# A table of relations made for two blocks at a time, one in each half of the array's rows, with four block buffers on the way out

## The chip, the cores and the metric

The kernel runs on one core of a Trainium2 chip. The metric is the device time of one execution in microseconds (us), lower is better; times given for a kernel are the median of several runs.

## What is computed

A graph network of four layers on 12500 nodes of 64 features and 400000 edges (sorted by target). Each layer normalises the nodes, takes the positive part, passes messages along the edges and adds the result to the nodes. The change touches what stands between the second layer and the third:

```python
h = jnp.maximum(_layernorm(x, axis=-1), 0.0)
x = x + _L1_gnn_ref(h, edge_attr_64, edge_index, M_W, M_b, U_W, U_b)   # ends in relu([H, Z] @ U_W.T + U_b)
h = jnp.maximum(_layernorm(x, axis=-1), 0.0)
x = x + _L2_gnn_ref(h, L2_gnn_weight, src, dst, edge_type_16)
# _L2: for r in range(16): msg = msg + h[src] * (etypes == r)[:, None] @ weight[r];  out = segment_sum(msg, dst)
```

The kernel does not multiply per edge. It makes a table with a row for every node and relation, `h @ weight[r]` for the 16 values of r, in device memory (HBM), and the third layer then gathers the row (node, relation) of each edge.

## The kernel before

Nodes are held in 98 blocks (`NB`) of 128 nodes, one node to a partition (`P` = 128), 64 words (`D`) a block. The program is a row of stages with a barrier between them: `starts_stage`, `record_stage` (which also makes the first layer's table), `gather_layer` for the first layer, `message_table`, `gather_layer` for the second, **`update_table`**, `gather_layer` for the third, and the stages of the fourth layer. Within a stage every engine runs an instruction list of its own, in the order in which it is written, and the lists are tied together by semaphores only. No scheduler moves anything.

`update_table` (line 865) has two parts. The first finishes the second layer and normalises: TensorE turns the sums and h of seven blocks (`turn`, L990 and L991, which write the two column halves, that is PSUM partitions 0 to 63 and 64 to 127), ScalarE copies them to `ct` (L950), TensorE multiplies by the update weights (`product`, L998), VectorE adds the bias, takes the positive part and adds to x (`update`, L907, L910), and VectorE and ScalarE normalise in chunks of 14 blocks (L925 to L940, L971, L977).

The second part is the loop over the 98 blocks that makes the table, which is the one that is changed:

- TensorE, `turn_h` (L1006): every seven blocks (`SUB`), seven matmuls with the identity turn h into `ps_t`, PSUM partitions 0 to 63.
- ScalarE, `turned_h` (L956): copies these 64x896 words to `ct[s % 2]`.
- TensorE, `table_block` (L1016): two matmuls a block with the 64 features as contraction, on array rows 0 to 63, give 1024 columns (16 relations of 64) in `ps_m[n % 2]`, 1024 words of PSUM, after both engines have taken the block before last out of it.
- `take_product`: ScalarE copies the first 512 columns (L961) and VectorE the other 512 (L915) to `tb[n % 2]`, each after the transfer of the block before last has landed (`s_out`).
- SP (L896): one transfer of 128x1024 words, 512 KB, to the table for each block, after both copies. Its queue holds nothing else in this part.

The weights `w` (64x1024 words) are loaded once, by SP at L892, ahead of the stage's first matmul. An f32 matmul has two records in the profile, so a block's two matmuls are four records of L1016.

## Time and profile before

| | |
|---|---|
| median of 3 runs | 22004.11 us (21988.52, 22004.11, 22110.69) |
| profiled execution | 22027.31 us, of which the span is 22025.5 us |
| mean granted TensorE clock over the span | 0.55 |
| busy: PE, DVE, ACT, POOL | 44%, 41%, 12%, 72% |
| DMA | 1898.85 MB, mean 86 GB/s |

The span is what lies between the first and the last instruction of the profiled execution. PE is TensorE's matmuls and PEld its weight loads, DVE is VectorE, ACT ScalarE, POOL GpSimd, SP SyncE, which issues most transfers. An engine's busy share is an average over all stages. "Idle before, released by" tells what an engine waited for; "issue" is time in which it waited for nothing that the profile shows. PEclk is the granted TensorE clock as a share of 2.4 GHz, 0.50 being 1.2 GHz. The stage `update_table` stands at 12577 to 12904 us of the span.

### The profile page before, as it was taken

The numbers are of one execution on the slowest core, as the hardware profiler recorded it, in microseconds if no ns is written. First come the engines' busy times: TensorE is split into PE (matmuls) and PEld (weight loads), VectorE is DVE, ScalarE is ACT, GpSimd is POOL, SyncE is SP. The second block draws the span as 40 slices with busy tenths as digits, with TensorE's granted clock in tenths as the row PEclk, the third lists the DMA queues.
The fourth block names the chain that finished last, engine by engine and source line by source line (L and its number), as shares of the span: only waits on it lengthen the run. The fifth ranks groups of instructions, "written<-read, shape, count | busy, mean of one in ns | idle before, by whom it ended". The sixth has DMA issues, their size and how long they took to land. (4 is left out here: it accounts for less than half of the span.)

```text
span 22025.5 us, 196973 instructions
## 1 busy us (share of the span) xinstructions
PE 9713.1 (44%) x45757; PEld 6967.4 (32%) x45758; DVE 9017.1 (41%) x22705; ACT 2705.0 (12%) x6341; POOL 15954.0 (72%) x16948
## 2 busy tenths in 40 slices
PE   2777776433333335666666653333333111111146
PEld 1333333233333334333333433333332000000046
DVE  7777777644444443222222232222223222222246
ACT  4000000000000000000000010000000222222256
POOL 2777777777777776777777647777776777777776
PEclk7555555555555555666666665555555555555578
DMA  3333332222222222222222132222222333333366
GB/s 109 98 99 98 99 97 82 72 63 63 61 62 63 63 62 58 60 63 63 63 60 63 46 134 63 61 63 63 63 61 59 111 110 111 110 112 111 109 208 232
DMA packets 1023243, 1898.85 MB, mean 86 GB/s; under 512 B 356036, under 2 KB 464484, under 8 KB 1009716
## 3 DMA queue, kind: packets, MB, share of 16 engines
q1 hardware_dynamic: 497556, 1233.35, 17.2%
q0 software_dynamic: 513696, 661.43, 11.3%
q10 hardware_dynamic: 11904, 3.04, 0.1%
q8 instruction: 38, 0.62, 0.0%
q14 instruction: 49, 0.40, 0.0%
HBM read 1385.02 MB, written 511.62 MB: 86 GB/s over the span
## 5 line engine op out<-in xcount | busy, mean ns | idle before, releaser
L1124 POOL DMA_INDIRECT arena<-table,arena x6464 | 6116.1, 946 | 2340.2 <-issue 1891.1
L1236 PE MATMUL psum<-arena 128*128 128x64 f32 x19392 | 3981.9, 391 | 5145.0 <-DMA arena<-table,arena 4548.8
L1236 PEld LDWEIGHTS psum<-arena 128*128 128x128 f32 x19392 | 3909.6, 304 | 5717.8 <-issue 5717.8
L1175 DVE TENSOR_TENSOR arena<-arena,psum 128x64 f32 x9696 | 2154.3, 222 | 8056.4 <-PE psum L1236 6827.4
L707 POOL DMA_INDIRECT rec<-arena x3125 | 3008.3, 963 | 1341.6 <-issue 949.4
L1320 POOL DMA_INDIRECT rec<-arena x3232 | 3109.5, 962 | 1069.2 <-issue 975.2
L1124 POOL DMA_INDIRECT arena<-ptable,arena x3232 | 3058.1, 946 | 1086.7 <-issue 985.7
L1403 PE MATMUL psum<-arena 128*128 x3232 | 589.1, 362 | 3512.0 <-DVE arena L1350 3433.1
L484 PE MATMUL psum<-arena 128*128 128x196 bf16 (+1 forms) x4375 | 1377.9, 428 | 1270.0 <-DVE arena L615 1270.0
L1222 PE MATMUL psum<-arena 128*128 128x512 f32 x808 | 838.0, 1141 | 1620.6 <-DMA arena<-ptable,arena 1620.6
L1403 PEld LDWEIGHTS psum<-arena 128*128 128x128 bf16 x3232 | 350.2, 108 | 3750.7 <-issue 3661.2
L1340 DVE TENSOR_TENSOR arena<-arena 128x136 f32<-128x136 f32 x404 | 122.1, 302 | 3058.3 <-DMA arena<-rec 3058.2
L615 DVE TENSOR_TENSOR arena<-psum,arena 128x392 f32<-128x392 f32 x1875 | 920.0, 491 | 345.6 <-PE psum L484 224.4
L484 PEld LDWEIGHTS psum<-arena 128*128 128x128 bf16 x4375 | 366.5, 115 | 2195.5 <-DVE arena L615 1820.0
L1154 DVE TENSOR_TENSOR arena<-psum,arena 128x1024 f32<-128x1024 f32 x808 | 984.5, 1219 | 23.4 <-issue 22.4
L1223 PE MATMUL psum<-arena 128*128 128x512 f32 x808 | 752.7, 1035 | 0.0
L1370 ACT ACTIVATE arena<-arena 128x1024 bf16<-128x1024 bf16 x404 | 463.4, 1147 | 2314.4 <-DMA arena<-lanes 2314.4
L620 DVE TENSOR_REDUCE arena<-arena 128x10 f32<-128x980 f32 x625 | 734.1, 1175 | 21.5
L1481 POOL TENSOR_SCALAR arena<-arena 128x128 bf16<-128x128 bf16 x880 | 641.3, 745 | 135.5 <-ACT arena L1493 133.2
L1222 PEld LDWEIGHTS psum<-arena 128*128 128x128 f32 x808 | 202.3, 311 | 1682.0 <-DMA arena<-ptable,arena 1517.9
L607 DVE TENSOR_TENSOR arena<-psum,arena 128x980 bf16<-128x980 f32 x625 | 729.9, 1168 | 0.0
L1198 ACT ACTIVATE arena<-psum 128x512 f32<-128x512 f32 x404 | 241.9, 599 | 3817.9 <-PE psum L1223 3817.9
(216 smaller groups left out, 11243.6 us busy)
## 6 DMA issues: line engine op xcount, KB each, us to landing
arena<-rec SPq DMA_DIRECT2D x303, 1408.0 KB
arena<-rec SPq DMA_DIRECT2D x440, 488.0 KB, 4.9
arena<-in_edge SPq DMA_DIRECT2D x625, 232.0 KB, 2.6
arena<-rec SPq DMA_DIRECT2D x404, 352.0 KB, 3.3
arena<-table,arena POOLq DMA_INDIRECT x6464, 2.4
arena<-lanes SPq DMA_DIRECT2D x101, 1024.0 KB
rec<-arena POOLq DMA_INDIRECT x6357, 2.3
table<-arena SPq DMA_DIRECT2D x196, 512.0 KB
```

The lines of the kernel that those rows point to most:

```text
L484: return nc.tensor.matmul(to, identb, one_hots, start=False, stop=False, skip_group_check=True)
L615: v.tensor_tensor(prod[g][:, 2 * n * WIDE:2 * n * WIDE + w], run[:, 0:w], buf[g][:, 2 * n * WIDE:2 * n * WIDE + w], ALU.mult).then_inc(s_s ...
L620: v.tensor_reduce(posf[:, g * CG * KEYS:(g + 1) * CG * KEYS], prod[g].rearrange("p (t w) -> p t w", w=NB), AX.X, ALU.add).then_inc(s_red, 1)
L707: nc.gpsimd.indirect_dma_start(rec, bass.IndirectOffsetOnAxis(ap=stage[g][:, j:j + 1], axis=0), recs[g][:, j * RW:(j + 1) * RW], None).the ...
L1124: nc.gpsimd.indirect_dma_start(rows[q][:, j * D:(j + 1) * D], None, tab, bass.IndirectOffsetOnAxis(ap=idx[:, j, field:field + 1], axis=0)) ...
L1154: v.tensor_tensor(ones, iotas, lanes, ALU.is_equal).then_inc(s_hot[q], 1)
L1175: v.tensor_tensor(block_sum, block_sum, ps[q % SB][:, j * D:(j + 1) * D], ALU.add).then_inc(s_add[j], 1)
L1222: nc.tensor.matmul(ps_q[q % 2], ident, rows[q], start=True, stop=False)
L1223: nc.tensor.matmul(ps_q[q % 2].rearrange("p (j f) -> p j f", f=D), ident, recs[q].rearrange("p (j w) -> p j w", w=RW)[:, :, R_Q:RW], start ...
L1236: last = nc.tensor.matmul(ps[q % SB][:, j * D:(j + 1) * D], hot[q % SB][:, j * P:(j + 1) * P], rows[q][:, j * D:(j + 1) * D], start=True, ...
L1320: nc.gpsimd.indirect_dma_start(slots, bass.IndirectOffsetOnAxis(ap=goal[q][:, j:j + 1], axis=0), rows[q][:, j * ROW:(j + 1) * ROW], None). ...
L1403: last = nc.tensor.matmul(ps_m[q % 2][:, j * 256:j * 256 + HW], hot_t[q % HB][:, j * P:(j + 1) * P], hparts[:, bass.ds(ats[j] * PARTS, HW) ...
```

## The change

Blocks are taken in pairs, seven blocks apart (block `n` and block `n + 7` of the same chunk of 14). The first block of a pair ("side 0") has its turned h on partitions 0 to 63 and the weights there, the second ("side 1") on partitions 64 to 127, where a second load puts the same weights. A unit `u` is one half (512 columns) of the rows of both blocks: two matmuls, one on array rows 0 to 63, the other on rows 64 to 127, into two banks of PSUM, each with its own semaphore `s_mm[side]`. Three such units fit in PSUM (`TRIO`), one of them where `ps_u` was, for which TensorE now waits at `s_pos`. ScalarE copies all of side 0 and VectorE all of side 1, one 128x512 copy a unit each. There are four block buffers `tb`, two for each side, and SP sends both blocks of a pair one after the other, every second unit. `turn_h` turns 14 blocks at a time, in the two column halves, and ScalarE's copy of them is 128x896.

```diff
--- before.py
+++ after.py
@@ -874,14 +874,17 @@
     uw, ub, w = b.take(D), b.take(D), b.take(width)
     ct = [b.take(SUB * P) for _ in range(2)]
     pos = [b.take(SUB * D) for _ in range(2)]
-    tb = [b.take(width) for _ in range(2)]
+    tb = [b.take(width) for _ in range(4)]
     assert b.at <= ARENA - NB * D
-    names = ("w", "t", "ct", "u", "pos", "x", "total", "mid", "sq", "var", "std", "rs", "h", "th", "ht", "mm")
-    s_w, s_t, s_ct, s_u, s_pos, s_x, s_total, s_mid, s_sq, s_var, s_std, s_rs, s_h, s_th, s_ht, s_mm = (sem("t2_" + n) for n in names)
-    s_ca, s_cv, s_out = ([sem(f"t2_{n}{k}") for k in range(2)] for n in ("ca", "cv", "out"))
+    names = ("w", "t", "ct", "u", "pos", "x", "total", "mid", "sq", "var", "std", "rs", "h", "th", "ht", "ca", "cv")
+    s_w, s_t, s_ct, s_u, s_pos, s_x, s_total, s_mid, s_sq, s_var, s_std, s_rs, s_h, s_th, s_ht, s_ca, s_cv = (sem("t2_" + n) for n in names)
+    s_mm = [sem(f"t2_mm{k}") for k in range(2)]
+    s_out = [sem(f"t2_out{k}") for k in range(4)]
     ps_t = psum[:, 0:SUB * P]
     ps_u = [psum[:, 1024 + 512 * k:1024 + 512 * k + SUB * D] for k in range(2)]
-    ps_m = [psum[:, 2048 + 1024 * k:3072 + 1024 * k] for k in range(2)]
+    TRIO = 3
+    ps_m = [[psum[:, 1024 * u + 512 * k:1024 * u + 512 * (k + 1)] for k in range(2)] for u in range(1, TRIO + 1)]
+    PAIRS_K = NB // 2
     bias = ub.rearrange("p (o f) -> p o f", o=1).to_broadcast([P, SUB, D])
 
     with nc.Block() as block:
@@ -889,13 +892,15 @@
         def _(sp):
             sp.dma_start(uw, a["uw"]).then_inc(s_w, 16)
             sp.dma_start(ub, a["ub"].to_broadcast([P, D])).then_inc(s_w, 16)
-            sp.dma_start(w[0:D, :], a["w2"]).then_inc(s_w, 16)
-            for n in range(NB):
-                sp.wait_ge(s_ca[n % 2], n // 2 + 1)
-                sp.wait_ge(s_cv[n % 2], n // 2 + 1)
-                sp.dma_start(dest[n * P:(n + 1) * P, :], tb[n % 2]).then_inc(s_out[n % 2], 16)
             for k in range(2):
-                sp.wait_ge(s_out[k], 16 * (NB // 2))
+                sp.dma_start(w[k * D:(k + 1) * D, :], a["w2"]).then_inc(s_w, 16)
+            for t in range(PAIRS_K):
+                for k, taken in ((0, s_ca), (1, s_cv)):
+                    n = t // SUB * CH + k * SUB + t % SUB
+                    sp.wait_ge(taken, 2 * t + 2)
+                    sp.dma_start(dest[n * P:(n + 1) * P, :], tb[t % 2 * 2 + k]).then_inc(s_out[t % 2 * 2 + k], 16)
+            for k in range(4):
+                sp.wait_ge(s_out[k], 16 * (-(-(PAIRS_K - k // 2) // 2)))
 
         @block.vector
         def _(dve):
@@ -909,12 +914,14 @@
                 dve.wait_ge(s_pos, s + 1)
                 v.scalar_tensor_tensor(x[:, at], pos[s % 2], 0.0, x[:, at], ALU.max, ALU.add).then_inc(s_x, 1)
 
-            def take_product(n):
-                dve.wait_ge(s_mm, n + 1)
-                wait_earlier(dve, s_out[n % 2], n // 2 * 16)
-                v.tensor_copy(tb[n % 2][:, half:], ps_m[n % 2][:, half:]).then_inc(s_cv[n % 2], 1)
-
-            dve.wait_ge(s_w, 48)
+            def take_product(u):
+                t, c = u // 2, u % 2 * half
+                dve.wait_ge(s_mm[1], u + 1)
+                if c == 0:
+                    wait_earlier(dve, s_out[t % 2 * 2 + 1], t // 2 * 16)
+                v.tensor_copy(tb[t % 2 * 2 + 1][:, c:c + half], ps_m[u % TRIO][1]).then_inc(s_cv, 1)
+
+            dve.wait_ge(s_w, 64)
             update(0)
             update(1)
             for k in range(CHUNKS + 2):
@@ -939,8 +946,8 @@
                     dve.wait_ge(s_rs, k - 1)
                     v.scalar_tensor_tensor(rows_of(h, k - 2, CH), rows_of(h, k - 2, CH), 0.0, spread(rs, k - 2),
                                            ALU.max, ALU.mult).then_inc(s_h, 1)
-            for n in range(NB):
-                take_product(n)
+            for u in range(NB):
+                take_product(u)
 
         @block.scalar
         def _(act):
@@ -949,16 +956,19 @@
                 wait_earlier(act, s_u, s - 1)
                 nc.scalar.copy(ct[s % 2], ps_t).then_inc(s_ct, 1)
 
-            def turned_h(s):
-                act.wait_ge(s_th, s + 1)
-
-                wait_earlier(act, s_mm, (s - 1) * SUB)
-                nc.scalar.copy(ct[s % 2][0:D, :], ps_t[0:D, :]).then_inc(s_ht, 1)
-
-            def take_product(n):
-                act.wait_ge(s_mm, n + 1)
-                wait_earlier(act, s_out[n % 2], n // 2 * 16)
-                nc.scalar.copy(tb[n % 2][:, 0:half], ps_m[n % 2][:, 0:half]).then_inc(s_ca[n % 2], 1)
+            def turned_h(k):
+                act.wait_ge(s_th, k + 1)
+
+                for side in range(2):
+                    wait_earlier(act, s_mm[side], (k - 1) * CH)
+                nc.scalar.copy(ct[k % 2], ps_t).then_inc(s_ht, 1)
+
+            def take_product(u):
+                t, c = u // 2, u % 2 * half
+                act.wait_ge(s_mm[0], u + 1)
+                if c == 0:
+                    wait_earlier(act, s_out[t % 2 * 2], t // 2 * 16)
+                nc.scalar.copy(tb[t % 2 * 2][:, c:c + half], ps_m[u % TRIO][0]).then_inc(s_ca, 1)
 
             turned(0)
             turned(1)
@@ -976,10 +986,10 @@
                     act.wait_ge(s_var, k)
                     nc.scalar.activation(rs[:, at], var[:, at], ACT.Sqrt, bias=epsc, scale=1.0 / D).then_inc(s_std, 1)
             turned_h(0)
-            for n in range(NB):
-                if n % SUB == SUB - 2 and n // SUB + 1 < SUBS:
-                    turned_h(n // SUB + 1)
-                take_product(n)
+            for u in range(NB):
+                if u % CH == CH - 4 and u // CH + 1 < CHUNKS:
+                    turned_h(u // CH + 1)
+                take_product(u)
 
         @block.tensor
         def _(pe):
@@ -998,37 +1008,39 @@
                     last = nc.tensor.matmul(ps_u[s % 2][:, j * D:(j + 1) * D], ct[s % 2][:, j * P:(j + 1) * P], uw, start=True, stop=True)
                 last.then_inc(s_u, 1)
 
-            def turn_h(s):
-                pe.wait_ge(s_h, s // 2 + 1)
-                wait_earlier(pe, s_ht, s)
+            def turn_h(k):
+                pe.wait_ge(s_h, k + 1)
+                wait_earlier(pe, s_ht, k)
                 for j in range(SUB):
-                    n = s * SUB + j
-                    last = nc.tensor.matmul(ps_t[0:D, j * P:(j + 1) * P], h[:, n * D:(n + 1) * D], ident, start=True, stop=True)
+                    for side in range(2):
+                        n = k * CH + side * SUB + j
+                        last = nc.tensor.matmul(ps_t[side * D:(side + 1) * D, j * P:(j + 1) * P], h[:, n * D:(n + 1) * D], ident, start=True, stop=True)
                 last.then_inc(s_th, 1)
 
-            def table_block(n):
-                s, j = n // SUB, n % SUB
-                if j == 0:
-                    pe.wait_ge(s_ht, s + 1)
-                wait_earlier(pe, s_ca[n % 2], n // 2)
-                wait_earlier(pe, s_cv[n % 2], n // 2)
-                for c in (0, half):
-                    last = nc.tensor.matmul(ps_m[n % 2][:, c:c + half], ct[s % 2][0:D, j * P:(j + 1) * P], w[0:D, c:c + half],
-                                            start=True, stop=True)
-                last.then_inc(s_mm, 1)
-
-            pe.wait_ge(s_w, 48)
+            def table_unit(u):
+                k, j, c = u // CH, u % CH // 2, u % 2 * half
+                if u % CH == 0:
+                    pe.wait_ge(s_ht, k + 1)
+                wait_earlier(pe, s_ca, u - TRIO + 1)
+                wait_earlier(pe, s_cv, u - TRIO + 1)
+                for side in range(2):
+                    rows = slice(side * D, (side + 1) * D)
+                    nc.tensor.matmul(ps_m[u % TRIO][side], ct[k % 2][rows, j * P:(j + 1) * P], w[rows, c:c + half],
+                                     start=True, stop=True).then_inc(s_mm[side], 1)
+
+            pe.wait_ge(s_w, 64)
             turn(0)
             for s in range(SUBS):
                 if s + 1 < SUBS:
                     turn(s + 1)
                 product(s)
             pe.wait_ge(s_ct, SUBS)
+            pe.wait_ge(s_pos, SUBS)
             turn_h(0)
-            for n in range(NB):
-                table_block(n)
-                if n % SUB == SUB - 3 and n // SUB + 1 < SUBS:
-                    turn_h(n // SUB + 1)
+            for u in range(NB):
+                table_unit(u)
+                if u % CH == CH - 6 and u // CH + 1 < CHUNKS:
+                    turn_h(u // CH + 1)
 
 
 def parts_stage(nc, sem, b, epsc, x, acc, h, hparts):
```

The order of TensorE's instructions in the table loop, which sets how often it turns and how many matmuls stand between. L1006 turns h and L1016 makes the table; the first row is the last product of the part before. Before:

```order
L998 MATMUL psum<-arena 128x64 x14
L1006 MATMUL psum<-arena 64x128 x7
L1016 MATMUL psum<-arena 128x512 x10
L1006 MATMUL psum<-arena 64x128 x7
L1016 MATMUL psum<-arena 128x512 x14
L1006 MATMUL psum<-arena 64x128 x7
L1016 MATMUL psum<-arena 128x512 x14
```

And with the change, where L1017 turns h and L1028 makes the table:

```order
L1008 MATMUL psum<-arena 128x64 x14
L1017 MATMUL psum<-arena 64x128 x14
L1028 MATMUL psum<-arena 128x512 x18
L1017 MATMUL psum<-arena 64x128 x14
L1028 MATMUL psum<-arena 128x512 x28
L1017 MATMUL psum<-arena 64x128 x14
L1028 MATMUL psum<-arena 128x512 x28
```

The turns are half as many and twice as long, and the second of them comes after 9 units (18 matmuls) where it came after 5 blocks (10 matmuls). The number of table matmuls is the same, 196.

The order of ScalarE's instructions from the last square roots of the normalisation on. L956 copies the turned h, L961 one half of a block. Before:

```order
L971 ACTIVATE arena<-arena 128x896
L977 ACTIVATE arena<-arena 128x14 x2
L956 COPY arena<-psum 64x896
L961 COPY arena<-psum 128x512 x5
L956 COPY arena<-psum 64x896
L961 COPY arena<-psum 128x512 x7
```

And with the change, L964 and L971 in their places:

```order
L981 ACTIVATE arena<-arena 128x896
L987 ACTIVATE arena<-arena 128x14 x2
L964 COPY arena<-psum 128x896
L971 COPY arena<-psum 128x512 x10
L964 COPY arena<-psum 128x896
L971 COPY arena<-psum 128x512 x14
```

The copies of products are as many as before, and those of the turned h half as many with twice the partitions. The first of them stands behind the same square root.

## Rows read from the trace of the kernel before

**Rows 1.** Timeline, start of the loop: start us, us, engine, line, operation [idle before].

```profile
12695.26 0.88 ACT L956 COPY arena<-psum 64x896 f32<-64x896 f32 x1
...
12696.20 16.57 PE L1016 MATMUL psum<-arena 64*128 64x512 f32 x19 [6.35 <-ACT arena L956]
...
12700.79 10.56 SPq L896 DMA_DIRECT2D table<-arena  x4
...
12713.56 3.16 PE L1006 MATMUL psum<-arena 128*64 128x128 f32 x14
```

**Rows 2.** Timeline, last transfer of the table and first of the next stage.

```profile
12900.62 0.33 SPq L896 DMA_DIRECT2D table<-arena  x1
12904.28 1.50 SPq L1110 DMA_DIRECT2D arena<-rec  x3
```

**Rows 3.** First line of the page.

```profile
span 22025.5 us, 196973 instructions
```

**Rows 4.** The page's costliest group: count, busy, mean ns, idle before and why.

```profile
L1124 POOL DMA_INDIRECT arena<-table,arena x6464 | 6116.1, 946 | 2340.2 <-issue 1891.1
```

**Rows 5.** Windows: length, busy PE, PEld, DVE, ACT, POOL; PEclk, DMA share, GB/s.

```profile
12696.20:12716.50 20.30, 20.30 (x34) 9.33 (x34) 4.79 (x8) 2.93 (x5) 0.00 (x0) 0.50 0.32 129
12716.50:12900.80 184.30, 183.03 (x542) 86.01 (x540) 64.32 (x93) 65.67 (x106) 0.00 (x0) 1.00 0.65 262
2000.00:3000.00 1000.00, 711.11 (x2242) 370.97 (x2242) 740.04 (x1678) 96.06 (x538) 759.39 (x791) 0.50 0.32 98
21932.50:22000.50 68.00, 67.58 (x425) 47.98 (x423) 43.83 (x45) 30.78 (x36) 9.15 (x4) 1.00 0.10 21
```

**Rows 6.** Timeline of TensorE in the steady part of the loop.

```profile
12784.73 1.74 PE L1006 MATMUL psum<-arena 128*64 128x128 f32 x14
12786.41 12.28 PE L1016 MATMUL psum<-arena 64*128 64x512 f32 x28
...
12800.29 12.28 PE L1016 MATMUL psum<-arena 64*128 64x512 f32 x28
...
12883.82 15.71 PE L1016 MATMUL psum<-arena 64*128 64x512 f32 x36
```

**Rows 7.** Lines from 12560 to 12905: count, busy, mean ns, idle before by releaser.

```profile
L915 DVE COPY arena<-psum 128x512 f32<-128x512 f32 x98 | 67.8, 692 | 135.2 <-DMA table<-arena 69.8 <-PE psum L1016 65.4
```

**Rows 8.** Timeline, two issues of SP, and two copies that waited for them.

```profile
12763.59 0.33 SPq L896 DMA_DIRECT2D table<-arena  x1
...
12764.83 0.33 SPq L896 DMA_DIRECT2D table<-arena  x1
...
12766.40 0.59 ACT L961 COPY arena<-psum 128x512 f32<-128x512 f32 x1 [1.76 <-DMA table<-arena]
...
12767.58 0.59 ACT L961 COPY arena<-psum 128x512 f32<-128x512 f32 x1 [0.59 <-DMA table<-arena]
```

**Rows 9.** DMA queues from 12780 to 12880: packets, MB, share of 16 engines.

```profile
q1 hardware_dynamic: 7232, 26.35, 64.9%
```

**Rows 10.** Timeline of TensorE, column halves at full clock in the stage's first part.

```profile
12608.79 0.27 PE L990 MATMUL psum<-arena 128*64 128x128 f32 x1
12608.80 0.27 PE L991 MATMUL psum<-arena 128*64 128x128 f32 x1
12608.90 0.27 PE L990 MATMUL psum<-arena 128*64 128x128 f32 x1
```

**Rows 11.** Lines from 12560 to 12905, copies of turned blocks; timeline, last bias addition.

```profile
L950 ACT COPY arena<-psum 128x896 f32<-128x896 f32 x14 | 12.6, 899 | 41.9 <-PE psum L991 41.9
L956 ACT COPY arena<-psum 64x896 f32<-64x896 f32 x14 | 12.6, 899 | 9.3 <-PE psum L1006 9.3
...
12687.20 0.62 DVE L907 TENSOR_TENSOR arena<-psum,arena 128x448 f32<-128x448 f32 x1 [5.12 <-PE psum L998]
```

**Rows 12.** DMA queue from 98 to 148; GB/s in 40 slices from 12796 to 12806.

```profile
q1 hardware_dynamic: 10465, 18.18, 101.5%
...
GB/s 377 426 410 230 393 410 442 410 393 49 0 0 197 410 393 426 393 279 426 410 393 393 410 66 33 0 0 0 0 0 0 213 410 393 410 393 279 0 246 393
```

## The prediction

> **What bounds the kernel now.** I looked first at how much of the program the change can reach, then at what paces that piece. The loop that makes the table of relations in `update_table` begins with ScalarE's copy of the first turned h at 12695.26 [rows 1] and ends with the next stage's first load at 12904.28 [rows 2]: 209.0 us, 0.95% of the span of 22025.5 us [rows 3]. The layer after it is one of the two whose indirect loads are the page's costliest group, 946 ns each on POOL and "issue" as the main reason for its idle time [rows 4], and nothing there is touched. The two gather layers and the scatter stage run as before, so the whole result lies inside these 209.0 us, and a change of 0.5% (110 us, about what a measurement of this kernel can tell from none) would take more than half of them.
>
> Inside, TensorE is the pace. In the stretch at full clock it is busy 183.03 of 184.30 us [rows 5]. A block is two f32 matmuls of 512 columns, each recorded twice, so four records: 28 records last 12.28 us and 36 last 15.71, which is 0.429 us a record and 1.72 us a block; the seven turns of h between cost 1.74 us, and 12786.41 to 12800.29 makes 13.88 us for seven blocks, 1.98 us a block [rows 6]. At the start the granted clock is 0.50 (1.2 GHz) until just after the first turn [rows 5], and a record takes twice that, 0.857 us (19 of them in 16.57, with the last one's tail) [rows 1]. VectorE's copy is 0.69 us a block [rows 7] and ScalarE's 0.59 [rows 8], so neither is near. The transfers are nearer: in 100 us they moved 26.35 MB and took 64.9% of the 16 engines [rows 9]. The waits put half of the copies' idle time on the table's DMA [rows 7], because a block's buffer is reused every second block, but a TensorE that is busy throughout does not wait for those copies: the DMA is next in line, not first.
>
> **The change, part by part.** *Row halves.* Work is now counted in units: one unit is a half row of 512 columns for two blocks, block A on array rows 0 to 63 and block B on rows 64 to 127, into different banks. There are 98 units with 196 matmuls, as many as before. If the two run at once a unit takes 0.857 us at full clock; if in turn, 1.71. No row here has two row halves. The nearest are the column halves of L990 and L991: they start 0.01 us apart and the pair advances by 0.11 us, no more than one 128-column record alone needs at that clock (1.74 us for 14 records of L1006) [rows 10, 6]. I take them as simultaneous and keep 1.71 as the other end.
>
> *Turns.* 14 turns of 7 matmuls become 7 turns of 14, as column pairs; by the column pairs a turn costs about 1.7 us, so six inside the loop instead of thirteen. TensorE then needs 14 x 0.857 + 1.7 = 13.7 us for 14 units, 0.98 us a unit.
>
> *Copies.* Each engine still makes 98 copies of 128x512, now each for its own block, so 0.69 us a unit is VectorE's need. ScalarE's copy of the turned h grows from 64 to 128 partitions; L956 and L950, of either height, both take 0.90 us [rows 11], so nothing is added, and there are seven fewer, on an engine with slack.
>
> *Transfers, the new pace.* The 98 transfers of 512 KB stay. From [rows 9], 26.35 MB at 64.9% is 406 GB/s at full use, 1.29 us a transfer. That exceeds TensorE's 0.98 and VectorE's 0.69. Does the queue stay full with four buffers? A transfer's buffer is free 2.8 us after its issue (issued 12763.59 and 12764.83, copies let go at 12766.40 and 12767.58) [rows 8]. Those two were issued 1.24 us apart and let their copies go 1.18 apart, so transfers overlap. The second of a pair starts some 0.33 us (one issue) after the first and queues behind its packets, 1.29 - 0.33 = 0.96 us more. The buffer is refilled by two copies, 1.38 us, plus 0.1 to the next issue. The ring is 2.8 + 0.96 + 1.38 + 0.1 = 5.24 us for two pairs, 2.62 us a pair; the packets alone want 2.58. They nearly coincide, and I take 2.63, so 49 pairs are 128.9 us. The ends: packets alone, 126.4, and for the upper end the longest full-use writes in this trace, 18.18 MB in 50 us or 364 GB/s with the engines full [rows 12], 1.44 us a transfer or 141.1 us.
>
> By the Trainium skill ("DMA: Bandwidth & Descriptors", Specifications) the HBM limit of a core is about 358 GB/s: 1.46 us a transfer, and the sum would be 143.5 us for the 98. Its neighbour here is the 364 GB/s; against it, the table's own packets show slices of 410 GB/s within a block [rows 12], and those 50 us are of packets of 1.7 KB, so I stay with 406.
>
> *Start and end.* The first two units take as long as the first block now if the halves run at once (two times two records at 0.857), so the first issue stays at 12700.79, 5.53 us after 12695.26 [rows 1]. While the clock is still at 1.2 GHz a pair takes 3.41 us on TensorE, 0.8 more than the transfers want. Two or three such pairs cost 2 us; bounds 0 and 5 (six pairs, until 12716.5). At the end, last issue to next stage is 12900.62 to 12904.28, 3.66 us, of which 1.29 is the transfer: 2.37 fixed [rows 2].
>
> *Added waits.* TensorE now waits for VectorE's last read of `ps_u` before the first turn, since `ps_m` reuses that PSUM: that read ends at 12687.82 [rows 11]. The turn's product isn't wanted before ScalarE's copy at 12695.26 [rows 1], which stands behind ScalarE's own share of the normalisation: 7 us of cover, more than the 3.16 us that a turn takes at 1.2 GHz [rows 1]. If that cover went, the wait would cost at most the length of this one read, 0.62 us. The weights are loaded a second time, 256 KB more on SP's queue ahead of TensorE's first matmul: one issue of 0.33 us [rows 2] and half a block's packets behind those of the first half, at most 0.65 us. I take 0.6; the ends are nothing and 1.
>
> *Sum.* 5.53 + 128.9 + 2.0 + 2.37 = 138.8, plus 0.6 for the weights, 139.4 us against 209.0: 70 us less, 0.32%. The profiled execution took 22027.3 us and would take 21957. The median of the three runs is 22004.1, 23 us lower; the same 70 us off it gives **21934 us**.
>
> **The rivals.** *The halves run in turn* (the change then does not do what it says on the array): 98 x 1.71 = 168.0, six turns 10.4, the first nine units at 1.2 GHz 15.4 more and their turn 1.4, start and end 6.8: 202 us, 7 less, 21997 us. For it: no row here shows row halves. Against: column halves do run at once.
>
> *The clock.* TensorE would now wait for transfers a third of the time. In the stretch from 2000 to 3000 us it is busy 711 of 1000 us with short waits and the clock stays 0.50; where it holds 1.00 near the end it is busy 67.58 of 68.00 us [rows 5]. At 1.2 GHz throughout, 98 x 1.71 + six turns of 3.16 + 6.8 = 193 us: 16 less, 21988 us; for half of the time 21961. Against it: at 1.2 GHz TensorE would be the pace again and busy all the time, which is the state in which the clock rose at 12716.5, and both halves of the array would be at work. The Trainium skill ("TensorE: Matmul & The Clock Gate", A second HAM failure mode) says that cycling through PSUM buffers with short idle times makes the clock swing. By that rule this rival would hold; the long stretch of the record stage agrees.
>
> *Slower writes*, 364 GB/s when the queue never empties: 141.1 + 10.5 = 152 us, 57 less, 21947 us.
>
> *Slower than before:* the two transfers of a pair, issued together, do not overlap but each pays its whole latency, about 2.5 us: 98 x 2.5 + 5.5 + 2.4 = 253 us, 44 more, 22048 us. It decides against the change from 2.03 us a transfer ((209.0 - 10.5) / 98). Against it stand the two overlapping ones of [rows 8].
>
> **How the numbers follow.** Forecast 0.60, slower writes 0.10, clock 0.12, halves in turn 0.12, no overlap 0.02, and 0.04 for runs that scatter (21988.5 to 22110.7 before). The forecast alone reaches from 76 us less (packets alone, no slow start) to 57. For 8 in 10 I take in the clock and most of the halves-in-turn case above, and below the 16 us by which the fastest run lies under the median: 21905 to 22000. None of the cases reaches 110 us of gain, since 98 transfers at 1.29 alone are 126 of the 209 us. Faster by over 0.5% can come by scatter only, 0.05; slower by over 0.5%, 0.02; the rest 0.93.
>
> **What the changed profile would show.** Right: the stage at about 139 us; DMA share above 0.9 and some 380 GB/s or more; the two sides' records of the unit starting together, 0.43 us apart from the next; copies let go by the DMA; TensorE some two thirds busy at clock 1.00 with a rise before 12716; POOL's layer after it unchanged. Wrong: records of one side starting when the other's end (halves in turn), PEclk falling within the loop, a DMA share near 0.6, or a stage time that differs while the total moves elsewhere.

## The result and the profile after

The changed kernel takes 21923.09 us (median of 8 runs, 21909.29 to 21929.95); the kernel before takes 22004.27 us beside it (8 runs, 21988.52 to 22122.10). The ratio is 0.9951 (95% interval 0.9932 to 0.9970): faster, by 81 us between the medians, where 70 were forecast. The ratio goes by means, and two of the eight runs before, near 22115 us, draw it below the 0.9963 of the medians.

The start and the end of the table loop in the changed kernel's timeline, in the columns of [rows 1] and [rows 2]:

```profile
12682.15 0.89 ACT L964 COPY arena<-psum 128x896 f32<-128x896 f32 x1
...
12683.08 7.44 PE L1028 MATMUL psum<-arena 64*128 64x512 f32 x26 [5.03 <-ACT arena L964]
...
12687.31 0.83 SPq L901 DMA_DIRECT2D table<-arena  x2
...
12814.02 1.58 SPq L901 DMA_DIRECT2D table<-arena  x2
12819.92 2.75 SPq L1122 DMA_DIRECT2D arena<-rec  x3
```

From 12682.15 to 12819.92 the loop takes 137.8 us, against 209.0 from [rows 1, 2]: 71.2 us less. Its steady part on TensorE, to be held against [rows 6]:

```profile
12738.64 1.99 PE L1028 MATMUL psum<-arena 64*128 64x512 f32 x8 [1.52 <-DVE arena L922]
12741.11 1.99 PE L1028 MATMUL psum<-arena 64*128 64x512 f32 x8 [0.48 <-DVE arena L922]
12743.55 1.99 PE L1028 MATMUL psum<-arena 64*128 64x512 f32 x8 [0.46 <-DVE arena L922]
```

Eight records, two units with four matmuls, last 1.99 us with the tail of the last; in [rows 6] eight records last over 3.4. The two row halves run at once, and TensorE then waits for a copy. Two windows of the loop (columns as in [rows 5]), SP's queue from 12700 to 12800 (as in [rows 9]) and the longest waits (waiter, what it waited for, us in total, times, longest):

```profile
12683.00:12686.30 3.30, 3.21 (x8) 1.52 (x10) 2.11 (x4) 0.62 (x2) 0.00 (x0) 0.50 0.00 0
12686.30:12816.00 129.70, 104.05 (x554) 45.37 (x550) 62.66 (x97) 60.78 (x103) 0.00 (x0) 1.00 0.98 390
...
q1 hardware_dynamic: 10739, 39.14, 98.0%
...
DVE arena L922 <- DMA table<-arena: 62.7, 46, 3.1
ACT arena L971 <- DMA table<-arena: 53.7, 44, 3.1
```

The transfers use 98% of the DMA engines where they used 64.9% [rows 9], TensorE is busy 104 of 130 us where it was busy throughout [rows 5], and its clock is 1.00 from 12686.3, eight records into the loop, where it came at 12716.5. The copies now wait for the DMA nearly alone: 62.7 of VectorE's 67.4 us, against 69.8 of 135.2 [rows 7].

The other 10 us lie elsewhere, nearly all in one stage, the source sums. The first and the last start of the source sums' matmuls (before at L1520, changed at L1532; durations in ns) and VectorE's waits that are put down to issue in that stage, before first:

```profile
L1520 PE MATMUL psum<-arena x10560: 197/201/273, 21153.1 to 21915.1; 128*128 128x81 bf16 x200
...
DVE arena L1455 <- issue: 189.3, 55, 3.7
```

```profile
L1532 PE MATMUL psum<-arena x10560: 197/201/273, 21062.2 to 21815.7; 128*128 128x81 bf16 x200
...
DVE arena L1467 <- issue: 182.9, 55, 3.4
```

762.0 us became 753.5, in a stage whose code is the same; from its first instruction to the next stage's first, as it is given below, 773.1 became 764.4. The profiled executions differ by more than the medians, 100.6 us of span; the rest is scatter between executions (a gather layer takes 4050 to 4060 us in different profiles of the same kernel, and the message table, the same code everywhere, 77 to 90).

### The profile page after: what moved, and what is told of

Its sections match the earlier page's. It is cut to its first block and busy times, and to the rows that moved or that the text cites. A ratio compares the mean times of both kernels' runs of the same rounds, so it can differ in the third digit from the quotient of the medians.

```text
span 21924.9 us, 196757 instructions
## 1 busy us (share of the span) xinstructions
PE 9616.3 (44%) x45757; PEld 6913.5 (32%) x45758; DVE 9016.1 (41%) x22705; ACT 2696.1 (12%) x6334; POOL 15934.1 (73%) x16948
```

## The experiments

Runs e5 to e8 were made on another chip, on which the kernel before takes 25873.7 us and the gather layers are slower; there only differences count. Runs e9 to e12 were made on yet another, on which it takes 21979.6. "The loop" is from ScalarE's first copy of turned h to the next stage's first load, as above. The kernel before ran beside the others each time.

**e1: the kernel before again.**

> The kernel before once more, for a second profile of it. The two profiles so far differ by 100.6 us in span, the medians by 81.2 us, and the table loop by 71.2 us (209.0 to 137.8). Theory: the loop gives the 71 us and the rest is scatter of the stages paced by POOL and of single executions; then this profile shows the loop at 209 +- 1 us, and its other stages differ from those of the first profile by up to 5 us each, in both directions. Rival: the change also shortens the stages after it (gather layers 4059.9 to 4055.6, source sums 773.1 to 764.4); then this profile repeats 4059.9 and 773.1 within 1 us.

Ratio 1.0008 (0.9995 to 1.0021). The loop takes 209.07 us, to 0.1 us what it took. The gather layers fall from 4060.1 and 4059.9 us to 4051.1 and 4050.7, so those are scatter, though of 9 us and both one way, more than the 5 that I expected. The source sums take 774.0 us (773.1 before), so that part of the rival, 773 against 764, was not dismissed; e10 to e16 are about it.

**e2: row halves, with two block buffers.**

```diff
...
-    tb = [b.take(width) for _ in range(4)]
+    tb = [b.take(width) for _ in range(2)]
...
-                    sp.dma_start(dest[n * P:(n + 1) * P, :], tb[t % 2 * 2 + k]).then_inc(s_out[t % 2 * 2 + k], 16)
+                    sp.dma_start(dest[n * P:(n + 1) * P, :], tb[k]).then_inc(s_out[k], 16)
...
-                    wait_earlier(act, s_out[t % 2 * 2], t // 2 * 16)
+                    wait_earlier(act, s_out[0], t * 16)
...
```

> The changed kernel with two block buffers (one a side) in place of four: row halves alone. Theory (the queue is kept full only by the second pair of buffers): the ring of 2.8 + 0.96 + 1.38 + 0.1 = 5.24 us now holds one pair, 49 x 5.24 + 10 = 267 us for the loop, some 58 us slower than the kernel before: 22062 us. Rival (the row halves alone bring the gain, the buffers are cover): loop 138 to 150 us, 21925 to 21940 us.

21970.1 us, 13 under the kernel before (ratio 0.9994, 0.9985 to 1.0004, which does not leave 1 out). The loop takes 210.4 us, which is neither the rival's 138 to 150 nor the theory's 267: the row halves alone bring nothing, but they cost nothing either, so the ring is not 5.24 us long. Its timeline (copies; side 1 is VectorE's, issued at 12731.33, side 0 ScalarE's, issued at 12732.88):

```profile
12731.33 0.33 SPq L901 DMA_DIRECT2D table<-arena  x1
...
12732.88 0.33 SPq L901 DMA_DIRECT2D table<-arena  x1
...
12734.44 1.29 DVE L922 COPY arena<-psum 128x512 f32<-128x512 f32 x2 [3.14 <-DMA table<-arena]
...
12735.99 0.59 ACT L971 COPY arena<-psum 128x512 f32<-128x512 f32 x1 [3.13 <-DMA table<-arena]
...
12738.46 1.29 DVE L922 COPY arena<-psum 128x512 f32<-128x512 f32 x2 [2.73 <-DMA table<-arena]
```

VectorE's two copies start 4.02 us apart: 1.3 us for the copies up to the next issue, and some 2.7 to 3.1 from an issue to the copy that it lets go (12731.33 to 12734.44). The two sides are issued 1.55 us apart. They are not a pair that leaves together: each side is a ring of its own, and the 0.96 us behind the partner's packets, which I had put into the ring, goes for the most part. The clock is of note here too:

```profile
12720.00:12820.00 100.00, 63.73 (x279) 26.02 (x277) 30.91 (x48) 29.30 (x51) 0.00 (x0) 0.87 0.62 252
```

With TensorE busy 64 of 100 us in this stretch it was granted 1.2 GHz for part of the time (0.87): the granted clock is 1.00 from 12708.5 to 12718.7, 0.50 to 12722.1, 1.00 to 12735.8, 0.50 to 12739.2, and so on. The changed kernel, busy 80%, kept 2.4 GHz.

**e3: four block buffers, without the row halves.**

```diff
...
-                sp.dma_start(dest[n * P:(n + 1) * P, :], tb[n % 2]).then_inc(s_out[n % 2], 16)
+                sp.dma_start(dest[n * P:(n + 1) * P, :], tb[n % 4]).then_inc(s_out[n % 4], 16)
...
-                wait_earlier(act, s_out[n % 2], n // 2 * 16)
-                nc.scalar.copy(tb[n % 2][:, 0:half], ps_m[n % 2][:, 0:half]).then_inc(s_ca[n % 2], 1)
+                wait_earlier(act, s_out[n % 4], n // 4 * 16)
+                nc.scalar.copy(tb[n % 4][:, 0:half], ps_m[n % 2][:, 0:half]).then_inc(s_ca[n % 2], 1)
```

> The kernel before with four block buffers in place of two: the buffers alone. Theory (TensorE paces the loop before, 1.98 us a block with the turns): only the small waits of TensorE for copies go, loop 204 to 209 us, total within 5 us of before, 22000 us. Rival (the transfers' waits were the limit, as half of the copies' idle time suggests): loop 135 to 160 us, 21935 to 21955 us.

The buffers themselves and VectorE's lines change likewise. Ratio 0.9996 (0.9982 to 1.0010), loop 208.2 us, within the 204 to 209 of the theory. The DMA waits of [rows 7] cost nothing, as TensorE's busy share said. Either part alone leaves the loop at 208 to 210 us; together they make it 137.8.

**e4: the halves one after the other, a first try.**

```diff
                 for side in range(2):
+                    if side:
+                        pe.wait_ge(s_mm[0], u + 1)
                     rows = slice(side * D, (side + 1) * D)
```

> The changed kernel, in which TensorE starts side 1 of a unit only when side 0's semaphore has risen, so that the two row halves run one after the other. Theory (running at once is what the row halves bring): a unit takes 1.71 us and one semaphore's delay of about 0.35, 98 x 2.06 and the turns and ends, loop 215 to 230 us, 22010 to 22025 us, slower than before or equal. Rival (fewer turns and more buffers bring the gain): loop under 170 us, under 21965 us.

21910.4 us, ratio 0.9967 (0.9955 to 0.9980), loop 150.6 us. By its own numbers that is the rival's result, but the edit does not do what it says: side 1 of a unit waits for side 0, yet side 0 of the next unit may start beside it. The weight loads show it, four records every 1.26 us, and a unit whose halves ran in turn would need 1.71:

```profile
12722.21 0.37 PEld L1030 LDWEIGHTS psum<-arena 64*128 64x128 f32 x4 [0.89 <-PE psum L1030]
...
12723.47 0.37 PEld L1030 LDWEIGHTS psum<-arena 64*128 64x128 f32 x4 [0.89 <-PE psum L1030]
...
12724.73 0.37 PEld L1030 LDWEIGHTS psum<-arena 64*128 64x128 f32 x4 [0.89 <-PE psum L1030]
```

**e9: no shared array.** So the same question was asked again with matmuls that fill the array.

```diff
...
-                    rows = slice(side * D, (side + 1) * D)
-                    nc.tensor.matmul(ps_m[u % TRIO][side], ct[k % 2][rows, j * P:(j + 1) * P], w[rows, c:c + half],
+                    nc.tensor.matmul(ps_m[u % TRIO][side], ct[k % 2][:, j * P:(j + 1) * P], wz[side][:, c:c + half],
                                      start=True, stop=True).then_inc(s_mm[side], 1)
```

> The changed kernel with every table matmul on all 128 array rows: two copies of the weights, one with zeros in rows 64 to 127 for side 0, one with zeros in rows 0 to 63 for side 1. The two matmuls of a unit then can't share the array, and nothing else changes (the earlier try let side 1 of one unit run beside side 0 of the next and kept a loop of 150.6 us). Theory: a unit takes 2 x 0.857 = 1.71 us, 98 units 168.0, six turns 10.4, ends 6.8, a slow start of 0 to 5, so loop 185 to 192 us, 48 to 54 us slower than the changed kernel. Rival (fewer turns, buffers and PSUM units bring it, not the halves running at once): loop under 155 us.

21945.4 us, ratio 0.9974 (0.9957 to 0.9990), loop 187.3 us, as the theory says:

```profile
12752.93 12.28 PE L1032 MATMUL psum<-arena 128*128 128x512 f32 x28
```

28 records take 12.28 us, to the hundredth what they take in [rows 6]. Running at once is worth 49.5 of the loop's 71.2 us (187.3 against 137.8). What is left, 21.8 us from the kernel before to e9, the rows tell nearly apart. TensorE's two groups in the loop, in the kernel before and then in e9 (columns as in [rows 7]):

```profile
L1016 PE MATMUL psum<-arena 64*128 64x512 f32 x392 | 181.1, 618 | 6.4 <-ACT arena L956 6.4
L1006 PE MATMUL psum<-arena 128*64 128x128 f32 x182 | 24.1, 287 | 0.0
```

```profile
L1032 PE MATMUL psum<-arena 128*128 128x512 f32 x392 | 171.7, 598 | 5.0 <-ACT arena L969 5.0
L1022 PE MATMUL psum<-arena 128*64 128x128 f32 x168 | 10.5, 276 | 0.0
```

The same 392 records take 9.4 us less, since the clock is 1.00 from 3.2 us into e9's matmuls where it came after 20.3; the turns, in column pairs, take 13.6 us less. Together that is 23.0, 1.2 more than the loop shows.

**e5: half of each transfer.** Relations 8 to 15 are not sent, so the third layer works with another table.

```diff
-                    sp.dma_start(dest[n * P:(n + 1) * P, :], tb[t % 2 * 2 + k]).then_inc(s_out[t % 2 * 2 + k], 16)
+                    sp.dma_start(dest[n * P:(n + 1) * P, 0:half], tb[t % 2 * 2 + k][:, 0:half]).then_inc(s_out[t % 2 * 2 + k], 16)
```

> The changed kernel sends only relations 0 to 7 of each block, 256 KB a transfer in place of 512; relations 8 to 15 of the table keep what the first layer's table left there. Theory (the transfers pace the loop at 1.27 to 1.29 us): the pace falls to TensorE's 0.98 us a unit or a ring of about 4.0 us for two pairs, loop 98 x 1.0 + 10 = 103 to 112 us, 26 to 35 us less than the changed kernel: 21890 to 21897 us. Rival (the loop is paced by something else, PSUM or the copies): loop within 5 us of 138.

The loop takes 106.9 us, within the forecast; 31 us less than the changed kernel on the same chip (137.5, e8). The totals (25757.5 against 25790.2) agree, with a difference of 33. TensorE is busy again:

```profile
15285.60:15392.50 106.90, 100.91 (x560) 47.47 (x560) 66.45 (x101) 61.74 (x106) 0.00 (x0) 0.98 0.64 241
```

So the transfers pace the changed loop, and with half of their bytes gone TensorE does, at 1.03 us a unit (100.91 us for 98).

**e6: two units in PSUM.**

```diff
-    TRIO = 3
+    TRIO = 2
...
-    ps_m = [[psum[:, 1024 * u + 512 * k:1024 * u + 512 * (k + 1)] for k in range(2)] for u in range(1, TRIO + 1)]
+    ps_m = [[psum[:, 1024 * u + 512 * k:1024 * u + 512 * (k + 1)] for k in range(2)] for u in range(2, TRIO + 2)]
...
-            pe.wait_ge(s_pos, SUBS)
```

> The changed kernel with two units in PSUM in place of three, and without TensorE's wait for ps_u. Theory: two units give a ring of 0.86 (matmul) + 0.4 (to the copy) + 0.69 (copy) + 0.15 = 2.1 us for two units, 1.05 a unit, still under 1.29, so loop 138 to 142 us, total within 4 us of the changed kernel. Rival: the third unit is what keeps TensorE ahead of the transfers, loop 150 us or more.

Loop 145.7 us, between the theory's 138 to 142 and the rival's 150; the total is 21 us over e8, of which the loop is 8 (the rest is not explained; the runs of the two overlap). The third unit is worth 8 us. A ring of 2.1 us for two units would do on average, but ScalarE now waits 74.8 us in the loop for TensorE, against 13.5 in the changed kernel. The rows of e2 show copies in twos after a landing, for which TensorE has to be ahead; that this is the reason is argued, not shown.

**e8: the changed kernel again.**

> The changed kernel once more, beside the others and for a second profile. Theory: loop 137.8 +- 1 us, 78 to 84 us faster than before by the medians; other stages differ from the first profile by up to 5 us each.

Loop 137.5 us, 83.5 us under the kernel before by the medians, ratio 0.9972 (0.9962 to 0.9983), on a chip where the program takes 18% longer. The gain is the same in microseconds.

**e7 and e12: the table loop merged into the part before it.** With the transfers as the floor, what is left is to start them earlier. The first part of the stage moves nothing for 118 us (DMA share 0.01 in the window from 12577 to 12695). In e7 every engine does the 14 units of chunk k-3 between its steps for chunk k (VectorE's list shown; ScalarE and TensorE likewise, with buffers `hc` of their own for the turned h). In e12 a third unit uses the PSUM of `ps_u` from unit 44 on, behind a wait for its last reader.

```diff
...
+            for k in range(LAG, CHUNKS + LAG):
+                for j in range(CH):
+                    take_product((k - LAG) * CH + j)
+                    if j == 0:
+                        step_normal(k)
+                    if j == 2:
+                        step_update(k, 0)
+                    if j == 4:
+                        step_total(k)
+                    if j == 6:
+                        step_var(k)
+                    if j == 7:
+                        step_mid(k)
+                    if j == 9:
+                        step_update(k, 1)
...
```

> The changed kernel's table loop taken into the update and normalisation of later chunks: units of chunk k-3 between the update steps of chunk k on every engine, two units in PSUM, own buffers for the turned h. Theory (the transfers' 98 x 1.29 = 126 us are the floor and stand after 118 us of a part that moves almost nothing): the first transfer can start when chunk 0 is normalised, about 66 us after the stage's start in place of 123, so the stage falls from 255.5 us to 200 to 215, and the total to 21865 to 21885 us. Rival: VectorE (16.7 us of work for 14 units against 18 us of transfers) and the waits in order on every engine eat it: stage over 240 us.

> The merged kernel with the third PSUM unit put back from the fourth chunk's units on, when ps_u is free. Theory (two units cost 8 us of a whole loop, 145.7 against 137.5): about half of that, so stage 232 to 236 us where it was 238.1, and the total 0.4 to 0.5% under the kernel before. Rival: no difference in the stage within 1 us, since TensorE's own work for two parts is the pace there.

e7 takes 25758.9 us where the changed kernel takes 25790.2 and the one before 25873.7; its stage 238.1 us against 255.4. That beats both kernels, but it is 17 us and not the 40 or more I expected, though it stays under the rival's 240. e12 brings the stage to 228.3 us, 4 below the 232 to 236 that I expected, so half of the 8 us was too little, and the total to 21863.6 us, 116 under the kernel before beside it (ratio 0.9936, 0.9914 to 0.9958), the fastest here. The two windows of e12, before the first transfer and from it to the last:

```profile
12538.30:12610.30 72.00, 44.53 (x393) 40.80 (x393) 19.29 (x26) 11.08 (x15) 0.00 (x0) 0.64 0.04 9
12614.60:12762.00 147.40, 123.99 (x762) 60.06 (x758) 89.47 (x133) 68.15 (x116) 0.00 (x0) 0.99 0.86 341
```

The first transfer starts 76 us after the stage's start, ten later than I had reckoned, and the DMA is in use for 86%, not 98, while TensorE works for two parts (124 of 147 us busy).

**e10 and e11: a spare semaphore.** Here begins the question of the source sums.

```diff
+    sem("t2_spare")
```

> The kernel before with one more semaphore taken in this stage and used by nothing. The stage of the source sums took 773 to 775 us in three profiles of kernels with 22 or 24 semaphores in this stage and 760 to 766 us in seven with 21 or 23. Theory A (the numbers that later stages' semaphores get matter): source sums near 761 us, total 10 to 13 us faster than before. Theory B (something else of the layout, code or state): source sums stay at 773 to 775, total as before.

> The changed kernel with one more semaphore taken and unused, 24 in place of 23. Theory A: source sums 773 to 775 us, total 10 to 13 us slower than the changed kernel. Theory B: 760 to 766 us, total as the changed kernel. The loop 137 to 139 us in both.

e10: ratio 1.0000 (0.9982 to 1.0019), source sums 773.1 us (its one profiled execution has a loop of 215 us, 6 more than the others, and is itself 29 us above its median). e11: 21894.0 us, 86 under the kernel before, source sums 762.3, loop 137.5. Theory A falls: in both the source sums stay where they were.

**e13 to e16: the waits put back.** What else the new code changes for a later stage is the length of the engines' lists: it has fewer waits. The edit on each engine repeats a wait that has just been met, here VectorE's (e15); e13 has all three, e14 only SP's, e16 only ScalarE's.

```diff
                 dve.wait_ge(s_mm[1], u + 1)
+                if c:
+                    dve.wait_ge(s_mm[1], u + 1)
```

> The changed kernel, in whose table loop SP, VectorE and ScalarE wait a second time for what they have just waited for (98, 49 and 56 waits), as many as the kernel before had more in this stage. The loop is paced by the transfers and should stay at 137.5 +- 1.5 us. Theory C (the source sums' loop runs 12 us faster because the lists of instructions ahead of it are shorter): source sums back at 773 to 775 us, total 10 to 13 us slower than the changed kernel. Theory D (something else): source sums 760 to 765 us, total as the changed kernel.

> The same with SP's 98 waits alone. Under theory C, if SP's list is the one that matters: source sums 773 to 775 us; else 760 to 765.

> The same with VectorE's 49 waits alone. Under theory C, if VectorE's list is the one that matters (its longest waits in the source sums are put down to issue, up to 3.7 us each turn of the loop): source sums 773 to 775 us; else 760 to 765.

> The same with ScalarE's 56 waits alone. Under theory C, if ScalarE's list is the one that matters: source sums 773 to 775 us; else 760 to 765.

| | loop | source sums | median, and under the kernel before (21987.5) |
|---|---|---|---|
| e13, all | 138.3 | 773.4 | 21915.8, 72 |
| e14, SP | 137.8 | 761.6 | 21901.8, 86 |
| e15, VectorE | 137.9 | 775.3 | 21912.4, 75 |
| e16, ScalarE | 137.8 | 765.7 | 21908.4, 79 |

The changed kernel as it is did not run beside these four; e14 stands in for it. The source sums' matmuls and VectorE's issue waits, in e15 and then in e14:

```profile
L1534 PE MATMUL psum<-arena x10560: 197/201/273, 21036.9 to 21801.3; 128*128 128x81 bf16 x200
...
DVE arena L1469 <- issue: 189.8, 55, 3.8
```

```profile
L1533 PE MATMUL psum<-arena x10560: 197/202/274, 21040.0 to 21790.4; 128*128 128x81 bf16 x200
...
DVE arena L1468 <- issue: 183.4, 55, 3.4
```

49 repeated waits on VectorE, in a stage that stays at 137.9 us, go with 764.4 us of source sums, and 98 on SP with 750.4, by these rows; the medians differ by 10.6 us the same way. Theory C holds, and VectorE's list is the one. ScalarE's waits (e16) bring 4 us at most by the source sums, which is within what profiles of like kernels differ by.

## Why the prediction was right and where it was wrong

**The mechanism was right.** TensorE paced the loop and the DMA was next (e2, e3); column halves were a fair guide to row halves (e9 against the changed kernel); the pace is now the transfers' (e5). The rival of the halves in turn falls with e9, the clock's with the granted 1.00, and that of no overlap with the 98% share.

**The sum, term by term.** The forecast for the loop was 138.8 us, and it took 137.8. From the last issue (12815.26) to the next stage are 4.66 us; with the 2.37 fixed ones of the forecast taken off, 2.29 belong to the transfers.

| term | forecast | measured |
|---|---|---|
| to the first issue | 5.5 | 5.2 (12682.15 to 12687.31) |
| slow pairs | 2.0 | none |
| transfers | 128.9 | 130.2 (127.95 from first to last issue, and 2.29) |
| end | 2.4 | 2.4, taken from before |

That the sum fits is in part luck: the transfers took 1.3 us more, and the slow pairs did not come. The pace of 2.63 us a pair stood on two legs that nearly met, the ring and the packets, and both were off. The ring of 5.24 us for two pairs was wrong: with two buffers, where it holds one pair, e2 measures 4.0 to 4.2 us, and with four that would be 2.1 us a pair, less than the transfers need. Against that a transfer costs more than 1.29 us: 39.14 MB in 100 us is 391 GB/s, 1.34 us each, 2.68 us a pair (at the 98.0% share, 399 GB/s at full use). The 406 GB/s from a queue in use for 65% was a little high for a full one. The rival of slower writes, 364 GB/s, falls with it. The Trainium skill's limit of about 358 GB/s for a core ("DMA: Bandwidth & Descriptors", Specifications) is exceeded too: 391 GB/s were written for 100 us, on a chip with one core at work.

The slow pairs did not come, since the clock rose eight records into the loop and not after the turn. With TensorE busy 80% and waiting after each two units the clock stayed 1.00; in e2, busy 64%, it went back and forth and was 0.87 in the mean. The swing that the Trainium skill describes ("TensorE: Matmul & The Clock Gate", A second HAM failure mode) is thus seen in e2, though there TensorE's waits before a unit are of up to 3.2 us and end with copies that wait for the DMA, and not in the changed kernel. The stretch from 2000 to 3000 us, which I had counted for that rule, does not swing either: its clock stays at 0.50.

Three figures of the rivals and bounds do not come out as written, none of which moves the forecast: "start and end 6.8" is nowhere worked out, and the two terms of the sum give 7.9; a pair at 1.2 GHz is 3.43 us by four times 0.857; and packets alone without slow pairs are 75 us less, not 76.

The 0.6 us for the second weights are not seen: the stage's part before the loop took 117.7 us where it took 118.5, and in the other profiles with this part unmerged it varies from 117.6 to 124.8.

**The first wrong step** is the sentence that "the whole result lies inside these 209.0 us". The loop gives 71.2 of 81 to 86 us. The rest is in the source sums, a stage whose code, data and order are untouched: 8 to 13 us, since VectorE's list ahead of its loop lost 49 waits (e13, e15). I had listed what the change removes from the loop and had costed the waits only there; every other stage I had put at nothing because its code was the same. My last sign of being wrong, a total that moves elsewhere, is what came. e2 points the same way: its loop is 1.4 us longer than before, its source sums take 760.6 us, and its median is 13 us lower, though the interval of its ratio does not leave 1 out.

**The second** is the bound. I called 0.5% about what a measurement can tell from no change, and put 0.93 on "within 0.5%". The forecast of 0.32% was then a forecast of nothing to be seen, and it rested on the three runs before. But the eight runs of the changed kernel end at 21929.95 and those of the kernel before begin at 21988.52; the interval of the ratio leaves 1 out. What is measured, 0.37% by the medians, is a clear gain that the chances as given did not announce. It would have been one without the source sums too: 10 us more on each run of the changed kernel would still leave them all some 48 us below the fastest run before. The scatter that I read from three runs was one run of 22110.69; the other two were 16 us apart.

## What to carry to other kernels

When one resource is the pace and another is at 65%, neither a faster first nor more buffers for the second pays alone; here each left the loop at 209 us, and both together took a third off it. A ring is to be counted for each buffer's own chain, not for the group in which the code writes them. And a change of some 50 instructions on an engine's list can move a later hardware loop on that engine: where a total moves by more than its stage, compare the untouched loops stage by stage before looking for a reason.

## What the runs showed of the hardware that I had not expected

The time of a loop depends on the instructions ahead of it on VectorE's list. In the source sums VectorE waits at one place in each turn of the loop, 55 times, with "issue" as the reason: 189.3 us in total in the kernel before, 189.8 in e15 and 190.1 in e13, against 182.9 in the changed kernel and 183.4 in e14. Over all profiles the stage takes 773.1 to 775.3 us in the six profiles of kernels with the longer list and 760.1 to 765.7 in the twelve with the shorter one, of which four ran on the chip where the program is 18% longer.

The place can be named. It is where the code loads 16 registers from `blks`, at the start of a turn's first group of sums. The line's own view, in the kernel before (durations in ns):

```profile
L1448 DVEq TENSOR_LOAD <-arena x55: 3603/3618/3649, 21152.5 to 21903.9; - x55
```

The load takes 3.62 us in the changed kernel too, so it is not what became shorter. What moves is when it begins. The trace also holds the steps of VectorE's own sequencer (semaphore waits and register operations, DVEq in the views). Held against the same step in the other profiles, every turn looked at (48 in each profile) has one step, none that waits for another engine, that comes 0.12 us late. In the kernel before, e1, e10, e13 and e15 it is the step right ahead of the load; in e3, whose list has two waits fewer, the one right behind it; in the twelve profiles with the shorter list it is another one, in the middle of the turn. The first two places lie inside VectorE's wait at the load, the third does not. 55 times 0.12 us is 6 to 7 us, which is the difference of the issue waits; the other 4 to 7 us of the stage are not traced to a place. At the loop's turn itself VectorE waits 17.4 us in total in every kernel looked at, and the DMA queues of kind "instruction" moved 3 packets in 740 us of this stage in the kernel before and 5 in the changed one, so code fetched by DMA at each turn is not what is seen. Why one step is late, and whether a shift by another number of instructions helps or hurts, stays open.

Two f32 matmuls of 64 rows in the two halves of the array, into different banks of PSUM, ran at full overlap here: two units in 1.99 us with the tail, where two units on the whole array need 3.43 (e9).
